# Indirect DMAs of GpSimd for the rows of the feed-forward layers, with an accumulating scatter for the last sum

## The chip, the cores and the metric

The kernel runs on one core of one Trainium2 chip. The metric is device time in microseconds (us). The core has five engines with queues of their own: TensorE (PE), VectorE (DVE), ScalarE (ACT), GpSimd (POOL) and SyncE (SP, which here only issues DMAs).

## What is computed

The input x has 4 sequences of 1024 tokens of 256 float32 values. The reference is a residual chain of four layers:

```python
x = x + attention(layernorm(x))       # 16 heads of 16, rope, degree-4 polynomial scores, causal
x = x + ffn(layernorm(x))             # first feed-forward layer
x = x + silu(fftconv(layernorm(x)))   # long convolution over the batch axis of this layout: 4 taps
x = x + ffn(layernorm(x))             # second feed-forward layer, the same weights
```

The feed-forward layer is a mixture of 16 experts of 176 hidden units, of which each token uses its 6 likeliest by a softmax gate, and a shared expert of 352 units; each expert is `(silu(x @ w1g) * (x @ w1u)) @ w2`. The kernel computes all experts for all tokens and multiplies the hidden units by the combine weight, zero for an expert that isn't chosen.

## The kernel before

`attention` computes the first layer and stores it into x1 in DRAM. Then all engines meet at a barrier, and `feed_forward` does the other three layers.

**Tiles.** A feed-forward tile is 4 blocks of 128 tokens, one block from each sequence, with 256 values each: 512 KB. There are 8 such tiles (NT) in each feed-forward layer, so 16 in all (TT). The rows of tile n come from x1 for n < 8, else from x3, the result of the first feed-forward layer and the convolution.

**Chunks.** The hidden units of all experts are cut into 25 chunks of 128 (FC), 22 of them routed (FM). For chunk c, PE computes gate and up (`gate_up`, L1237, 12 matmuls of 128x512 as three products of high and low parts), ACT applies SiLU (L965), DVE multiplies by up (L1134) and by the combine weights `cbs` (L1137; no such factor in the last 3 chunks, L1139), ACT and DVE split the product into a high part `ah` (L969) and a low part `al` (L1143), and PE adds the second layer (`down`, L1253) one chunk later.

**Work spread over the chunks.** Between the chunks of tile n stand the prologue of tile n+1 and the epilogue of tile n-1. Prologue: statistics of `xp` in chunks 9 and 10 (L1083), the reciprocal deviation on POOL (`rstd_of`, L897 and L899), normalising `xp` in chunk 11 (L1075), transposes in chunks 12 and 14 (L1263), the split of the transposed rows (L946, L1092), gate logits, softmax and the choice of experts in chunks 16 to 24. Epilogue: the transposed result is added to the residual rows `xe` in chunks 4 and 6 (L1150). In a tile of the first layer ("convolution tile") `xe` is then normalised, POOL does the convolution (`convolve`, L908 to L916), ACT its SiLU in chunk 14, and DVE the sum in chunk 16 (L1194). In the second layer ("plain tile") the sum of L1150 is the output.

**SP's queue.** All DMAs are issued by SP in one order. `weights_out(n)` stores the combine weights of tile n (L833) and loads them back, broadcast, for chunks 0 to 2; then `turn(n)` loads the residual rows `xe` of tile n-1, loads the rows `xp` of tile n+1, loads `cbs` for chunks 3 to 20 (each when chunk c-3 is multiplied), stores `xe`, and loads `cbs` for chunk 21. Before the first tile SP loads `xp`, the identity, the gate weights, the taps and then the feed-forward weights chunk by chunk (`stage`), which ACT and DVE split during tile 0.

PE, DVE, ACT and POOL run the tiles as two straight ones, a loop of three pairs, two straight ones, a loop of two pairs, and two straight ones.

Of the kernel before, what the change touches and what calls it, by code (L numbers as in the profile page):

```python
# [18 lines left out]
ALU = mybir.AluOpType  # L19
AX = mybir.AxisListType  # L20

P = 128
# [11 lines left out]
ONE = 1  # L34
# [670 lines left out]
def feed_forward(nc, x1, w1, w2, gate, taps_in, ident_in, weights_t, x3, out):  # L705
# [5 lines left out]
    with ctx:  # L711
# [3 lines left out]
        def sem(name):  # L715
# [8 lines left out]
                  for c in range(FM)]  # L724
# [29 lines left out]
        pad = sb("f_pad", [P, 1])  # L754
        zero = sb("f_zero", [P, 1])
# [12 lines left out]
                   conv_link csilu x3 xp xe store link""".split()  # L768
# [35 lines left out]
        def _(sp):  # L804
# [3 lines left out]
            def load(to, n, second, name):  # L808

                sp.dma_start(to[:], rows(x3, n - NT) if second else rows(x1, n)).then_inc(s[name], 16)  # L810

            sp.sem_inc(s["store"], ONE)
            load(xp, 0, False, "xp")
# [27 lines left out]
            for c in range(RING, FC):  # L841
                if c < FM:
                    spread(0, c)
                if c + 1 < FC:
                    stage(c + 1)
                if c == 4:
                    sp.wait_ge(s["tx"], KE)
                    load(xp, 1, False, "xp")
# [24 lines left out]
            with sp.Fori(1, NT - 1) as n:  # L873
                turn(n, False, False, x3, True)
            turn(NT - 1, True, False, x3, True)
            turn(NT, True, False, x3, True)
            with sp.Fori(NT + 1, TT - 1) as n:
                turn(n, True, True, out, True)
            turn(TT - 1, True, True, out, False)
            turn(TT, True, True, out, False)  # L880
            sp.wait_ge(s["store"], ONE + 16 * TT)

        @block.gpsimd
        def _(pool):
# [34 lines left out]

            rstd_of(0, "pst", "peps", "prs", 0)  # L920

            def tile(n, parity, epilogue, prologue):
# [483 lines left out]
```

## Time and profile before

| | us |
|---|---|
| median of 3 runs | 2603.06 (2592.45 to 2606.33) |
| the profiled execution, its own time | 2598.01 |
| its span | 2596.3 |
| attention, from the span's start | to about 786 |
| feed-forward, 16 tiles | from about 786 to 2596.3 |
| PE busy in the span | 2329.8 |

The span is the profiled part of the execution; 1.7 us lie around it. The mean TensorE clock granted was 0.937 of full speed over the span. SP shows no busy time, since issuing a DMA isn't counted as busy. PE, DVE, ACT and POOL are given as busy time; a matmul of 128x512 shows about 0.4 us though two follow each other every 0.23 us, since they overlap.

### The profile page before, as it was taken

What the parts mean: (1) busy time and instruction counts of PE and PEld (TensorE: products, weight loads), DVE (VectorE), ACT (ScalarE), POOL (GpSimd) and SP (SyncE); (2) the same over time, 40 slices, a digit from 0 to 9 for tenths busy, and PEclk for the clock granted to TensorE, in tenths of its full rate; (3) what the DMA queues carried; (4) which work ended last, traced back from release to release, by engine and by line L of the source; (5) the groups of instructions that cost most, each with busy time, mean ns of one, the idle gap of its engine ahead of it and who ended that gap; (6) DMA issues with size and microseconds to landing.
All of it is one profiled execution on the core that took longest, in us unless ns stands there. A gap on an engine that the chain in (4) does not pass through costs nothing.

```text
span 2596.3 us, 32427 instructions
## 1 busy us (share of the span) xinstructions
PE 2329.8 (90%) x11472; PEld 1711.7 (66%) x11472; DVE 1484.4 (57%) x2605; ACT 1019.5 (39%) x1550; POOL 463.5 (18%) x590
## 2 busy tenths in 40 slices
PE   4776976786686999999999999999999999999998
PEld 3333533442334777787778778787888887888887
DVE  3656765755675655656465565656545454454554
ACT  2555655554463533233333323333333332333332
POOL 1434433443360002202020120202000000000000
PEclk8788888887787999999999999999999999999999
DMA  3133123213304421222212212221222212212121
GB/s 103 20 65 57 37 54 57 58 17 57 81 7 127 141 82 46 83 74 63 67 57 74 64 64 74 67 67 51 82 74 62 73 54 77 72 61 74 61 66 57
DMA packets 114098, 170.57 MB, mean 66 GB/s; under 512 B 18320, under 2 KB 58896, under 8 KB 113808
## 3 DMA queue, kind: packets, MB, share of 16 engines
q1 hardware_dynamic: 113936, 168.44, 23.3%
q8 instruction: 98, 1.61, 0.2%
q14 instruction: 64, 0.52, 0.1%
HBM read 130.10 MB, written 13.11 MB: 55 GB/s over the span
## 4 chain that ended last, share of the span: by engine, by line
PE 65%; DVE 3%; issue 1%; DMA 1%; ACT 0%; POOL 0%; DVEq 0%; ACTq 0%; POOLq 0%; SPq 0%
PE ffn_psum L1237 42%; PE ffn_psum L1253 21%; DVE xp L1075 1%; PE ffn_psum L1263 1%; PE ffn_psum L1290 1%; DVE pr L1137 1%; DVE al L1143 0%; DVE pr L1134 0%; DMA cbs<-weights_t 0%; PE ffn_psum L1273 0%; PE ffn_psum L1279 0%; DVE w1l L1058 0%; DMA xp<-x 0%; DMA weights_t<-z 0%; DVE w2l L1060 0%
## 5 line engine op out<-in xcount | busy, mean ns | idle before, releaser
L1237 PE MATMUL ffn_psum<-f_xh,w1h 128*128 128x512 f32 x1600 | 513.1, 401 | 8.6 <-issue 8.6
L1134 DVE TENSOR_TENSOR pr<-pr,ffn_psum 128x512 f32<-128x512 f32 x352 | 242.4, 689 | 485.4 <-PE ffn_psum L1237 422.7
L969 ACT ACTIVATE ah<-pr 128x512 fp32r<-128x512 f32 x400 | 252.6, 632 | 657.2 <-DVE pr L1137 599.7
L1237 PE MATMUL ffn_psum<-f_xl,w1h 128*128 128x512 f32 x1600 | 504.5, 396 | 0.0
L1237 PE MATMUL ffn_psum<-f_xh,w1l 128*128 128x512 f32 x1600 | 504.1, 396 | 0.0
L426 DVE TENSOR_TENSOR a<-a 128x1024 f32<-128x1024 f32 (+2 forms) x304 | 323.5, 1087 | 241.9 <-ACT a L330 240.8
L965 ACT ACTIVATE pr<-ffn_psum 128x512 f32<-128x512 f32 x400 | 238.8, 597 | 449.8 <-DVE al L1143 279.4
L330 ACT ACTIVATE a<-attn_psum 128x1024 f32<-128x1024 f32 (+1 forms) x320 | 290.6, 942 | 285.9 <-PE attn_psum L639 285.3
L1143 DVE TENSOR_TENSOR al<-pr,ah 128x512 fp32r<-128x512 f32 x400 | 284.8, 712 | 181.6 <-ACT ah L969 159.4
L1237 PEld LDWEIGHTS ffn_psum<-f_xl,w1h 128*128 128x128 f32 x1600 | 302.6, 189 | 74.5 <-issue 2.9
L1237 PEld LDWEIGHTS ffn_psum<-f_xh,w1l 128*128 128x128 f32 x1600 | 302.1, 189 | 72.0
L1237 PEld LDWEIGHTS ffn_psum<-f_xh,w1h 128*128 128x128 f32 x1600 | 295.4, 190 | 70.9 <-issue 7.2
L1253 PE MATMUL ffn_psum<-ah,w2h 128*128 128x512 f32 x800 | 319.1, 399 | 22.6 <-DVE al L1143 22.6
L1253 PE MATMUL ffn_psum<-ah,w2l 128*128 128x512 f32 x800 | 316.3, 395 | 0.0
L1253 PE MATMUL ffn_psum<-al,w2h 128*128 128x512 f32 x800 | 316.1, 395 | 0.0
L639 PE MATMUL attn_psum<-qt,kt 48*128 48x512 f32 (+3 forms) x768 | 148.4, 441 | 174.8 <-DMA kt<-sq 160.8
L897 POOL TENSOR_TENSOR f_rstd<-f_mv,f_eps 128x4 f32<-128x4 f32 x24 | 13.0, 541 | 1474.9 <-DVE f_mv L1064 1474.9
L639 PEld LDWEIGHTS attn_psum<-qt,kt 48*128 48x128 f32 x768 | 70.5, 205 | 297.5 <-DMA kt<-sq 164.5
L1137 DVE TENSOR_TENSOR pr<-pr,cbs 128x512 f32<-128x512 f32 x352 | 251.8, 715 | 25.5 <-DMA cbs<-weights_t 5.5
L298 POOL TENSOR_SCALAR_AFFINE_SELECT a<-a 128x256 f32<-128x256 f32 x256 | 180.0, 719 | 144.3 <-DVE a L426 134.8
L1253 PEld LDWEIGHTS ffn_psum<-ah,w2h 128*128 128x128 f32 x800 | 150.5, 188 | 68.0 <-DVE al L1143 31.9
L660 PE MATMUL attn_psum<-a,v 128*32 128x512 f32 (+3 forms) x1536 | 175.0, 546 | 7.0 <-POOL a L298 4.4
(157 smaller groups left out, 2028.8 us busy)
## 6 DMA issues: line engine op xcount, KB each, us to landing
cbs<-weights_t SPq DMA_DIRECT2D x128, 256.0 KB, 3.2
cbs<-weights_t SPq DMA_DIRECT2D x64, 224.0 KB, 2.9
cbs<-weights_t SPq DMA_DIRECT2D x64, 192.0 KB, 2.9
cbs<-weights_t SPq DMA_DIRECT2D x64, 160.0 KB, 2.5
qt<-sq SPq DMA_DIRECT2D x128, 64.0 KB, 2.3
kt<-sq SPq DMA_DIRECT2D x128, 64.0 KB, 2.3
xp<-x SPq DMA_DIRECT2D x16, 512.0 KB, 5.3
cbs<-weights_t SPq DMA_DIRECT2D x64, 128.0 KB, 2.8
```

The costliest lines, as they stand in the source:

```text
L298: last = pool.affine_select(out=d[:, :, k], in_=d[:, :, k], compare_op=ALU.is_ge, fill=0.0, base=0, pattern=[[0, 2], [1, P]], channel_mult ...
L330: act.activation(a[:, n % RA, :, 0:width(u)], S(n)[:, :, 0:width(u)], ACT.Square).then_inc(s_q1, 1)
L426: dve.tensor_tensor(t, t, t, ALU.mult).then_inc(s_a, 1)
L639: last = pe.matmul(S(n)[:, half, col:col + w], kt[lo:lo + 3 * D, unit % 2, c, j * P:(j + 1) * P], qt[lo:lo + 3 * D, unit % 2, c, tiles[0] ...
L660: last = pe.matmul(OT(qc)[32 * h:32 * h + 32, at_:at_ + w], v[:, b % 2, lo:lo + 32], a[:, (n - 1 + h // 2) % RA, h % 2, col:col + w], star ...
L965: act.activation(pr[:], GB(q), ACT.Silu).then_inc(s["silu"], 1)
L969: act.activation(ah[:, q % 2], pr[:], ACT.Copy).then_inc(s["ah"], 1)
L1134: dve.tensor_tensor(t, t, UB(q), ALU.mult).then_inc(s["p1"], 1)
L1137: dve.tensor_tensor(t, t, cbs[:, c % RING], ALU.mult).then_inc(s["p"], 1)
L1143: dve.tensor_tensor(al[:, q % 2], pr[:], ah[:, q % 2].bitcast(F32), ALU.subtract).then_inc(s["al"], 1)
L1237: last = pe.matmul(out, lhs(a, k), rhs(b, k), start=n == 0, stop=n == 3 * KE - 1)
L1253: last = pe.matmul(OB(m), w[:, c, m * P:(m + 1) * P], t[:, q % 2], start=c == 0 and j == 0, stop=c == FC - 1 and j == 2)
```

## The change

- SP no longer loads `xp`. POOL keeps a column of row numbers per block (`load_at`, 128 x 4, uint32), adds 128 to all of them for each tile (`next_index`), and gathers the rows with four indirect DMAs of 128 rows of 1 KB.
- SP no longer stores `xe`. POOL stores it with four scattering indirect DMAs, with row numbers of its own (`store_at`). For the second layer these accumulate onto `out`.
- For that, SP copies the residual rows of the tile from x3 to `out` in DRAM where it loaded them into `xe`, and DVE copies the second layer's result from PSUM into `xe` instead of adding it.
- At the start of the feed-forward part SP issues a copy of the whole of x1 into x3, as the first entry of its queue. Only the first scatter waits for it.
- POOL's tiles are written out one by one, not looped. DVE waits for 64 per tile on the rows' semaphore (four DMAs of 16), SP for 64 per tile on the stores'.

```diff
-            sp.sem_inc(s["store"], ONE)
-            load(xp, 0, False, "xp")
+            sp.dma_start(x3, x1).then_inc(s["init"], 16)
             sp.dma_start(ident[:], ident_in).then_inc(s["const"], 16)
...
-            def turn(n, loads_second, residual_second, store_to, prologue):
-                sp.wait_ge(s["store"], ONE + 16 * (n - 1))
-                load(xe, n - 1, residual_second, "xe")
-                if prologue:
-                    sp.wait_ge(s["tx"], KE * (n + 1))
-                    load(xp, n + 1, loads_second, "xp")
+            def turn(n, residual_second, prologue):
+                if not (isinstance(n, int) and n == 1):
+                    sp.wait_ge(s["store"], 16 * B * (n - 1))
+                if residual_second:
+                    sp.dma_start(rows(out, n - 1 - NT), rows(x3, n - 1 - NT)).then_inc(s["xe"], 16)
+                else:
+                    sp.dma_start(xe[:], rows(x1, n - 1)).then_inc(s["xe"], 16)
...
-                if store_to is x3:
-                    sp.wait_ge(s["x3"], n)
-                    sp.dma_start(rows(x3, n - 1), xe[:]).then_inc(s["store"], 16)
-                else:
-                    sp.wait_ge(s["x2"], 2 * n)
-                    sp.dma_start(rows(out, n - 1 - NT), xe[:]).then_inc(s["store"], 16)
...
+            def next_index(to):
+                pool.tensor_tensor(to[:], to[:], step[:], ALU.add).then_inc(s["index"], 1)
+
+            def gather(dram, indexed):
+                pool.wait_ge(s["index"], indexed)
+                for b in range(B):
+                    pool.indirect_dma_start(xp[:, b], None, flat(dram), bass.IndirectOffsetOnAxis(load_at[:, b:b + 1], 0)
+                                            ).then_inc(s["xp"], 16)
+
+            def scatter(dram, indexed, **how):
+                pool.wait_ge(s["index"], indexed)
+                for b in range(B):
+                    pool.indirect_dma_start(flat(dram), bass.IndirectOffsetOnAxis(store_at[:, b:b + 1], 0), xe[:, b], None,
+                                            **how).then_inc(s["store"], 16)
...
+            for n in range(TT + 1):
+                if n < TT - 1:
+                    pool.wait_ge(s["tx"], KE * (n + 1))
+                    if n >= 2:
+                        pool.wait_ge(s["store"], 16 * B * (n - 1))
+                    if n + 1 == NT:
+                        first_index(load_at)
+                    else:
+                        next_index(load_at)
+                    gather(x1 if n + 1 < NT else x3, 2 * n + 2 + (n == 0))
+                if 1 <= n <= NT:
                     rstd_of(1, "cst", "ceps", "crs", n - 1)
-                if prologue:
+                if n < TT - 1:
                     rstd_of(0, "pst", "peps", "prs", n + 1)
-                if epilogue == "conv":
+                if 1 <= n <= NT:
                     convolve(n - 1)
+                    pool.wait_ge(s["x3"], n)
+                elif n:
+                    pool.wait_ge(s["x2"], 2 * n)
+                if n:
+                    if n in (1, NT + 1):
+                        first_index(store_at)
+                    else:
+                        next_index(store_at)
+                    to = 2 * n + 3 if n < TT - 1 else n + TT + 1
+                    if n == 1:
+                        pool.wait_ge(s["init"], 16)
+                    if n <= NT:
+                        scatter(x3, to)
+                    else:
+                        scatter(out, to, compute_op=ALU.add)
...
-                    dve.wait_ge(s["xp"], 16 * m + 16)
+                    dve.wait_ge(s["xp"], 16 * B * (m + 1))
...
-                dve.tensor_tensor(t, t, X.rearrange("p (b e) -> p b e", e=E), ALU.add).then_inc(s["x2"], 1)
+                y = X.rearrange("p (b e) -> p b e", e=E)
+                if plain:
+                    dve.tensor_copy(t, y).then_inc(s["x2"], 1)
+                else:
+                    dve.tensor_tensor(t, t, y, ALU.add).then_inc(s["x2"], 1)
```

## Rows read from the trace of the kernel before

**Rows 1.** The page, parts 1 and 4: busy time, and the chain's shares.
```profile
PE 2329.8 (90%) x11472; PEld 1711.7 (66%) x11472; DVE 1484.4 (57%) x2605; ACT 1019.5 (39%) x1550; POOL 463.5 (18%) x590
...
PE 65%; DVE 3%; issue 1%; DMA 1%; ACT 0%; POOL 0%; DVEq 0%; ACTq 0%; POOLq 0%; SPq 0%
```

**Rows 2.** Windows, convolution tile and plain tile: length, busy, clock, DMA share, GB/s.
```profile
1041.00:1152.00 111.00, 109.36 (x483) 87.98 (x482) 64.85 (x124) 37.50 (x62) 17.29 (x20) 1.00 0.22 68
...
1929.00:2038.00 109.00, 109.00 (x483) 88.23 (x482) 57.04 (x110) 36.76 (x62) 1.56 (x2) 1.00 0.22 68
```

**Rows 3.** Timeline at the feed-forward's start: start us, us, engine, what [idle before].
```profile
786.28 0.38 SPq L810 DMA_DIRECT2D xp<-x  x1
...
787.26 0.42 SPq L815 DMA_DIRECT2D pr<-gate  x1
...
790.78 1.41 DVE L1083 BATCH_NORM_STATS2 f_stats<-xp 128x6 f32<-128x256 f32 x4 [7.23 <-DMA xp<-x]
...
791.18 0.32 ACT L936 ACTIVATE gt_h<-pr 128x144 fp32r<-128x144 f32 x1 [12.32 <-DMA pr<-gate]
...
794.08 1.38 DVE L1075 TENSOR_SCALAR xp<-xp,f_mv,f_rstd 128x256 f32<-128x256 f32 x4 [1.28 <-POOL f_rstd L899]
...
794.59 0.26 ACT L983 ACTIVATE z<-z 128x64 f32<-128x64 f32 x1
...
796.73 0.60 ACT L946 ACTIVATE f_xh<-ffn_psum 128x512 fp32r<-128x512 f32 x1 [1.88 <-PE ffn_psum L1263]
```

**Rows 4.** Timeline of SP's queue: the combine weights' store, three tiles.
```profile
2147.21 0.31 SPq L833 DMA_DIRECT2D weights_t<-z  x1
...
2260.93 0.31 SPq L833 DMA_DIRECT2D weights_t<-z  x1
...
2369.72 0.31 SPq L833 DMA_DIRECT2D weights_t<-z  x1
```

**Rows 5.** Timeline where PE, DVE and ACT jump back in their loops.
```profile
1264.05 0.40 SPq L810 DMA_DIRECT2D xp<-x  x1
...
1270.12 0.69 DVE L1143 TENSOR_TENSOR al<-pr,ah 128x512 fp32r<-128x512 f32 x1 [5.02 <-issue]
```

**Rows 6.** Windows of two heavy loading stretches; last columns DMA share, GB/s.
```profile
4.00:8.00 4.00, 0.00 (x0) 0.00 (x0) 3.12 (x15) 0.00 (x0) 1.82 (x6) 1.00 1.09 410
...
788.00:790.00 2.00, 0.00 (x0) 0.00 (x0) 0.00 (x0) 0.00 (x0) 0.00 (x0) 0.50 0.94 308
```

**Rows 7.** The page, part 6: KB of one, median us from issue to landing.
```profile
xp<-x SPq DMA_DIRECT2D x16, 512.0 KB, 5.3
...
cbs<-weights_t SPq DMA_DIRECT2D x128, 256.0 KB, 3.2
...
affine<-ln_affine SPq DMA_DIRECT2D x8, 0.1 KB, 7.5
...
x<-xr SPq DMA_DIRECT2D x16, 256.0 KB, 2.3
```

**Rows 8.** Timeline of a plain tile: residual rows loaded, and first used.
```profile
1934.16 0.41 SPq L810 DMA_DIRECT2D xe<-x  x1
...
1952.84 0.68 DVE L1150 TENSOR_TENSOR xe<-xe,ffn_psum 128x512 f32<-128x512 f32 x1
```

**Rows 9.** Timeline of a convolution tile: Pool's first work, DVE's last sum.
```profile
1074.80 0.56 POOL L897 TENSOR_TENSOR f_rstd<-f_mv,f_eps 128x4 f32<-128x4 f32 x1 [81.47 <-DVE f_mv L1064]
...
1114.11 1.22 DVE L1194 TENSOR_TENSOR xe<-xe,z 128x1024 f32<-128x1024 f32 x1
```

**Rows 10.** Timeline: the four normalising instructions, convolution tile, then plain tile.
```profile
1090.82 3.19 DVE L1075 TENSOR_SCALAR xp<-xp,f_mv,f_rstd 128x256 f32<-128x256 f32 x4
...
2091.40 1.38 DVE L1075 TENSOR_SCALAR xp<-xp,f_mv,f_rstd 128x256 f32<-128x256 f32 x4
```

**Rows 11.** Timeline of the kernel's end.
```profile
2592.37 0.69 DVE L1150 TENSOR_TENSOR xe<-xe,ffn_psum 128x512 f32<-128x512 f32 x1 [1.20 <-PE ffn_psum L1290]
...
2593.09 0.39 SPq L867 DMA_DIRECT2D out<-xe  x1
```

More of the change, by code:

```diff
@@ L754, in feed_forward @@
         pad = sb("f_pad", [P, 1])
+        load_at = sb("load_at", [P, B], mybir.dt.uint32)
+        store_at = sb("store_at", [P, B], mybir.dt.uint32)
+        step = sb("step", [P, B], mybir.dt.uint32)
         zero = sb("f_zero", [P, 1])
@@ L767, in feed_forward @@
                    lgT lgS lgX sm ex comb cx cT cw g u silu p1 p ah al s2 oT back x2 cst ceps crs cy plink clink mx
-                   conv_link csilu x3 xp xe store link""".split()
+                   conv_link csilu x3 xp xe store link index init""".split()
         s = {n: sem("f_" + n) for n in names}
@@ L871, in turn @@
                     weights_out(n + 1)
[L873 to L876, printed above, removed]
+            turn(1, False, True)
+            with sp.Fori(2, NT + 1) as n:
+                turn(n, False, True)
             with sp.Fori(NT + 1, TT - 1) as n:
[L878 to L881, printed above, removed]
+                turn(n, True, True)
+            turn(TT - 1, True, False)
+            turn(TT, True, False)
+            sp.wait_ge(s["store"], 16 * B * TT)
         @block.gpsimd
@@ L918, in convolve, with first_index @@
                         links = links + 1
-            rstd_of(0, "pst", "peps", "prs", 0)
-            def tile(n, parity, epilogue, prologue):
-                if epilogue == "conv":
+            flat = lambda dram: dram.rearrange("b t p e -> (b t p) e")
+            def first_index(to):
+                pool.iota(to[:], [[N, B]], base=0, channel_multiplier=1).then_inc(s["index"], 1)
+            def next_index(to):
+                pool.tensor_tensor(to[:], to[:], step[:], ALU.add).then_inc(s["index"], 1)
@@ new lines, in _ @@
+            pool.iota(step[:], [[0, B]], base=P, channel_multiplier=0).then_inc(s["index"], 1)
+            first_index(load_at)
+            gather(x1, 2)
+            rstd_of(0, "pst", "peps", "prs", 0)
+            for n in range(TT + 1):
[4 more added lines that the diff above has]
+                    if n + 1 == NT:
+                        first_index(load_at)
+                    else:
+                        next_index(load_at)
+                    gather(x1 if n + 1 < NT else x3, 2 * n + 2 + (n == 0))
+                if 1 <= n <= NT:
@@ L924, in tile @@
                     rstd_of(1, "cst", "ceps", "crs", n - 1)
-                if prologue:
+                if n < TT - 1:
                     rstd_of(0, "pst", "peps", "prs", n + 1)
-                if epilogue == "conv":
+                if 1 <= n <= NT:
                     convolve(n - 1)
-            tiles(pool, tile)
+                    pool.wait_ge(s["x3"], n)
[13 more added lines that the diff above has]
+                        scatter(out, to, compute_op=ALU.add)
@@ L1143, in low_act, with residual @@
                 dve.tensor_tensor(al[:, q % 2], pr[:], ah[:, q % 2].bitcast(F32), ALU.subtract).then_inc(s["al"], 1)
-            def residual(e, half):
+            def residual(e, half, plain):
                 if half == 0:
@@ L1176, in tile @@
                     if epilogue and c in (4, 6):
-                        residual(n - 1, (c - 4) // 2)
+                        residual(n - 1, (c - 4) // 2, epilogue == "plain")
                     if epilogue == "conv":
@@ L1213, in _ @@
             for half in range(2):
-                residual(TT - 1, half)
+                residual(TT - 1, half, True)
         @block.tensor
```

5 lines of the change are left out of this document (removed).

## The prediction, on record before the changed kernel ran

> **What bounds the kernel now.** I read the page's busy shares and its chain first: PE is busy for 90% of the span and makes up 65% of the chain that ended last, and POOL has none of the chain [rows 1]. Then the windows of one tile of each kind: PE is busy for all 109 us of a plain tile, and for 109.36 of 111 us of a convolution tile, while the DMA engines are busy for 0.22 of it [rows 2]. So in the steady part only what makes PE wait counts, and moving rows on another queue changes nothing unless something arrives late. PE isn't the bound in three places: at the start of the feed-forward part [rows 3], where the loops jump back [rows 4, 5], and at the end [rows 11]. The change touches all three.
>
> **1. The copy of x1 into x3, first in SP's queue.** It is 4 x 8 x 128 x 256 float32 values, 4.19 MB, from DRAM to DRAM. Nobody waits for it until the first scatter, after chunk 16 of tile 1: that chunk is at 1114.1 us in tile 2 [rows 9], one tile of 110.8 us earlier in tile 1, so at 1003 us, 217 us after the start. By its own semaphore it is hidden. But behind it in the same queue stand the identity, the gate weights, the taps and the first chunks of w1 and w2, and the trace shows that a small transfer in this queue lands with the large ones ahead of it: the affine rows, 0.1 KB each, took 7.5 us at the median, where 256 KB took 3.2 us elsewhere [rows 7], and the gate weights were waited for until 791.18, 3.9 us after their issue, behind the 512 KB of `xp` [rows 3]. So I take it that the first weights arrive after the copy.
>
> How long is the copy? The highest rate shown is 410 GB/s, for loads from DRAM [rows 6]. The copy passes DRAM twice for each byte, so I halve it: 205 GB/s, 20.5 us. Nothing in the trace copies DRAM to DRAM, so the bounds are wide: at the full 410 GB/s 10.2 us, and at the slope between 256 KB in 3.2 us and 512 KB in 5.3 us (125 GB/s) [rows 7] 33.5 us. The latter two move pieces of 2 and 1 KB, the copy long runs, so I stay near the first.
>
> What is then late? The load of `xp` leaves this queue; at 308 GB/s [rows 6] it held it for 1.7 us. The weights move by 20.5 - 1.7 = 18.8 us. Behind them are two chains [rows 3]. Gate weights: ACT splits them at 791.18, DVE subtracts, and only then may it normalise; before, it sat idle for 1.28 us there, waiting for POOL, so 18.8 - 1.3 = 17.5 us remain. First w1 and w2: ACT splits them and the taps until 794.85, and starts on the transposed rows at 796.73, so there the slack is 1.9 us and 16.9 remain. The later one counts: **+17.5 us**, bounds +7.2 and +30.5 (10.2 and 33.5 less 3.0). Tile 0 can't win it back, since every stage of it follows these splits.
>
> The Trainium skill speaks on this. Its page "DMA: Bandwidth & Descriptors", section "Latency and other measured facts", gives copies between DRAM tensors 207 GB/s in each direction where the pitch isn't unlucky, and 103 to 164 where it is. By the first the copy would take 20.3 us and the sum stays; by the second 26 to 41 us, and the sum grows by 5 to 20 us. No row of this trace can decide between them.
>
> **2. The first gather.** POOL first writes three small constants and the row numbers, then issues four DMAs. The price of an indirect DMA on POOL is not in this trace. From below it is SP's issue of a plain one, 0.4 us [rows 3]; from above I put four times POOL's shortest step on two operands, 0.56 us [rows 9], so about 2 us, and rival D says what more would do. I take 1 us each. Then `xp` lands near 786.5 + 1 + 4 + 5 = 796.5 us, 6 us later than before. It lies under the 18.8 us of the gate weights, and costs nothing; without that cover it would be 4.5 us (6 less the 1.3 us).
>
> **3. Gathers and scatters in the steady part.** In a convolution tile x3's sum is ready at 1115.3 [rows 9]. POOL then adds to its row numbers, issues four scatters, waits for them to land, adds again and issues four gathers. What is queued behind these on POOL is the `rstd_of` of the convolution in the next tile, which DVE waits for: it comes at 1074.8 plus one tile of 110.8, so 1185.6 us. There are 70 us for eight DMAs and one landing of about 5.3 us: 13 us at 1 us each. In a plain tile the scatter follows chunk 10 and the gather chunk 14, and there are more than 80 us until the next chunk 10. `xp` is overwritten after its last transpose, as before, and the statistics need it in chunk 9 of the next tile. Cost 0, covered by PE's chunks; if the cover is gone, rival D.
>
> DVE and POOL do hinder each other: the four normalising instructions took 3.19 us beside POOL's convolution and 1.38 us in a plain tile, where POOL is idle [rows 10], and the convolution tile is the one in which PE idles 1.64 us [rows 2]. In plain tiles the scatter's four DMAs would now be issued just when chunk 11 normalises. If writing them hinders as the convolution does, it costs up to 1.64 us in each of 7 plain tiles, 11.5 us; if not, 0. POOL reads only 128 x 4 row numbers for it, so I go near the low end: **+2 us**.
>
> **4. SP's queue in the steady part.** In the first layer it loses the 512 KB of `xp`, at the place where the loops jump back. There DVE waited 5.02 us for its own instructions with this load just issued [rows 5], and the tile with the jump lasts 113.72 us where the next lasts 108.79 [rows 4]; 4.9 us more; there are three jumps. 512 KB are 1.7 us of the queue. If all of it delays the fetch, 3 x 1.7 = 5 us come back; if none, 0. I take **-1.5 us**. In the second layer the load of `xe` becomes a copy of the same size from x3 to out. It is issued at 1934.16 and first needed at 1952.84 [rows 8]: 18.7 us for a transfer that took 5.3 us as a load; twice that is still covered. DVE's copy out of PSUM replaces an addition with the same operand from PSUM: 0.
>
> **5. The end.** Before, the last addition ends at 2593.06, SP stores 512 KB, and the span ends at 2596.3, 3.2 us later [rows 11]. Now POOL waits for DVE, adds to its row numbers (0.56 us, the like at L897 [rows 9]), issues four DMAs at 1 us, and the last one has to land: 2.3 us as the 256 KB store [rows 7], more for reading first, say 3. Sum 7.6 instead of 3.2: **+4.5 us**. Bounds: +1 (0.4 us each, 2.3 to land: 4.4 less 3.2) and +10 (2 us each, 4.6 to land).
>
> **Sum.** 17.5 + 2 - 1.5 + 4.5 = +22.5 us on the profiled execution's 2598.0, so 2620.5. The median of the runs shown is 5.05 us above that execution, so the time is 2603.06 + 22.5 = **2625.6 us**, slower by 0.9%. All low ends together (7.2 + 0 - 5 + 1) give +3, all high ends (30.5 + 11.5 + 0 + 10) +52.
>
> **The rivals.**
> A. *The copy doesn't hold up the weights*, because it is fast or because the engines take from it only in between. This is the one on the other side: not slower. Then the first gather decides the start (+4.5, less up to 1.7 of queue time), and with the end the sum is 4.5 + 2 - 1.5 + 4.5 = +9.5, 2612.6 us, within 0.5%. It decides from where the delay is under 8 us, so the copy under 11 us or 380 GB/s. For it: 410 GB/s was seen. Against it: that was one pass through DRAM, and the order of landing in [rows 7].
> B. *The stall at the jumps goes away with `xp`'s load.* Three times 4.9, 14.8 us, in place of 1.5: +9.2, 2612.3 us, also within 0.5%. Against it: the five loads of `cbs` and the load of `xe` stay ahead of the fetch. Together with A it would be 2599 us, 0.1% faster, which no measurement tells.
> C. *The copy runs on few engines.* Its outermost dimension is 4, so if the transfer is cut along it, four engines of 16 carry it, at a quarter of the rate: 41 us at 410 GB/s to 82 us at 205. The delay is then 38 to 79 us and the time 2646 to 2687 us; middle 2666. Against it: both sides are one contiguous run, which may be cut in any way. The Trainium skill, page "DMA: Bandwidth & Descriptors", section "Rules for kernel authors", has this as a rule: an outermost dimension under 16 confines a DMA to that many engines. No DMA in this trace shows it.
> D. *POOL can't write its DMAs fast enough.* From 8.1 us for each ((70.3 - 5.3) / 8) the next `rstd_of` is late. At 10 us each it would be 15 us in each of 7 convolution tiles: +105, about 2730 us. For it: nothing but that the price is unknown.
> E. *Writing the DMAs hinders DVE's normalising* as the convolution does: 11.5 in place of 2, so 2635 us. The Trainium skill, page "SBUF — State Buffer", section "SBUF: two separate sides", says that one blocks the other, and that it is the DMA that waits behind DVE; by it the cost here is only a later scatter, and the sum would be 2 us less.
>
> **How the numbers follow.** Chances: forecast 0.60, A 0.13, B 0.05, A and B together 0.03, C 0.07, E 0.09, D 0.03. Change of 0.5% is 13 us, about what a measurement of this kernel tells from none. Slower by more: the forecast (all but 0.04 of it, for a copy near its lower bound), C, D and E, 0.75. Within it: A, B, both, and the 0.04, less 0.02, so 0.23. Faster by more: those 0.02, for both together with low ends elsewhere. Range: at the low end A and B reach to 2609; at the top the copy at its upper bound gives 2639, with E 2648, and C begins at 2646, so I go to 2655. Outside are D, most of C, and A and B together: under 2 in 10.
>
> **What would show it.** In the changed kernel's profile: a gap of about 30 us without PE from 783 us, ended by ACT waiting for the gate weights near 810 us (A: near 792, and DVE waiting for `xp`); SP's row of the copy with about 20 us to landing; tiles of 108.8 and 110.8 us as before; four normalising instructions in a plain tile of 1.4 us (E: 3.2); DVE's wait at the jump of 4 to 5 us (B: none); 7 to 8 us from the last copy of DVE to the end. The prediction is wrong above all if the weights are not held by the copy, or held much longer than 20 us.

## The result, and the profile after

The changed kernel takes 2614.03 us (median of 12 runs, 2605.38 to 2623.97), the kernel before 2602.94 (median of 12, 2592.45 to 2608.29): a ratio of 1.0047 with the interval [1.0027, 1.0066]. It is slower by 11 us (7 to 17). The forecast was 22.5 us slower; the time lies in the range, near its low end, and just inside "within 0.5%", a case that the forecast had given 0.23, against 0.75 for slower by more. It is also nearer to rival A's 2612.6 us than to the forecast's 2625.6, so the time alone can't say which of them is true; the profiles can.

Time was lost in two places, the start and the end, and little changed between them. To see that, the span is cut at events that both kernels have. The zero is the barrier between attention and feed-forward (POOL's first memset after it). Attention isn't touched by the change, yet its end lies between 779 and 792 us in the profiles of this study, so spans and single times carry up to 13 us that have nothing to do with an edit; stretches counted from the barrier don't.

| us | before | after | difference |
|---|---|---|---|
| barrier | 786.20 | 779.48 | -6.7 |
| barrier to DVE's statistics of `xp` | 4.58 | 16.70 | +12.1 |
| barrier to ACT's split of the gate weights | 4.98 | 17.09 | +12.1 |
| barrier to PE's first transpose | 9.41 | 21.50 | +12.1 |
| barrier to the first store of combine weights | 24.99 | 35.44 | +10.45 |
| tile 0, store to store | 115.61 | 115.32 | -0.3 |
| tiles 1 to 14 | 1551.76 | 1551.09 | -0.7 |
| the rest, to the end of DVE's last instruction | 114.50 | 114.35 | -0.15 |
| from there to the span's end | 3.24 | 10.72 | +7.5 |
| feed-forward, barrier to end | 1810.10 | 1826.92 | +16.8 |

By these profiles the feed-forward part is 16.8 us longer; the medians of whole runs say 11.1, with an interval that reaches 17. The profiles of the other runs weren't kept, so what lies between the two numbers isn't shown.

The page of the changed kernel, busy times (part 1), the queue of POOL's DMAs (part 3) and the chain's shares (part 4); [rows 1] are those of before:

```profile
PE 2315.5 (89%) x11472; PEld 1703.2 (65%) x11472; DVE 1485.1 (57%) x2605; ACT 1019.6 (39%) x1550; POOL 630.8 (24%) x751
...
q0 software_dynamic: 9216, 16.79, 2.8%
...
PE 64%; DVE 3%; issue 1%; DMA 1%; POOL 0%; ACT 0%; POOLq 0%; DVEq 0%; ACTq 0%
```

POOL does 167 us more work, and almost none of it is in the chain. The timeline of the changed kernel at the feed-forward's start, against [rows 3]:

```profile
779.49 0.59 SPq L811 DMA_DIRECT2D x<-x  x1
...
780.55 1.19 POOL L920 DMA_INDIRECT xp<-x,load_at  x1 [0.40 <-POOL load_at L912]
780.75 1.28 SPq L813 DMA_DIRECT2D pr<-gate  x1
782.04 0.96 POOL L920 DMA_INDIRECT xp<-x,load_at  x1 [0.30 <-issue]
...
784.56 0.95 POOL L920 DMA_INDIRECT xp<-x,load_at  x1 [0.30 <-issue]
796.18 1.41 DVE L1117 BATCH_NORM_STATS2 f_stats<-xp 128x6 f32<-128x256 f32 x4 [19.34 <-DMA xp<-x,load_at]
796.57 0.32 ACT L970 ACTIVATE gt_h<-pr 128x144 fp32r<-128x144 f32 x1 [25.93 <-DMA pr<-gate]
...
799.45 1.38 DVE L1109 TENSOR_SCALAR xp<-xp,f_mv,f_rstd 128x256 f32<-128x256 f32 x4 [1.25 <-POOL f_rstd L888]
...
800.98 1.08 PE L1301 MATMUL ffn_psum<-f_ident,xp 128*128 128x128 f32 x4 [24.93 <-DVE xp L1109]
```

Two things are late: ACT waits for the gate weights (the issue at 780.75), and DVE for the gathered `xp`, although the gathers stand in POOL's own queue and were issued by 785.5. The one that decides is `xp`. Before it normalises, DVE still waits 1.25 us for POOL's reciprocal deviation, as before (1.28 in [rows 3]), and that hangs on the statistics of `xp`; the gate weights have been used by then. The landings (the page's DMA issues: KB, median us) say the same, against [rows 7]:

```profile
out<-x SPq DMA_DIRECT2D x8, 512.0 KB, 4.6
...
xp<-x,load_at POOLq DMA_INDIRECT x64, 3.2
...
x<-xe,store_at POOLq DMA_INDIRECT x32, 2.5
out<-xe,store_at POOLq DMA_INDIRECT x32, 4.7
...
pr<-gate SPq DMA_DIRECT2D x1, 72.0 KB, 15.8
...
x<-x SPq DMA_DIRECT2D x1, 15.5
```

The copy landed 15.5 us after its issue: 4.19 MB / 15.5 us = 270 GB/s. The gate weights landed after it. Windows of the same stretch (us, PE, PEld, DVE, ACT, POOL, clock, DMA share, GB/s): the DMA share is 1 or more for 8 us, then the rate falls to 124 GB/s. A share of 1.40 can't be meant as it stands, so I take 507 GB/s as a matter of how a window counts long pieces, and only the whole landing as a rate.

```profile
779.50:783.50 4.00, 0.00 (x0) 0.00 (x0) 0.00 (x0) 0.00 (x0) 2.91 (x11) 0.50 0.74 264
783.50:787.50 4.00, 0.00 (x0) 0.00 (x0) 0.00 (x0) 0.00 (x0) 1.71 (x2) 0.50 1.40 507
787.50:791.50 4.00, 0.00 (x0) 0.00 (x0) 0.00 (x0) 0.00 (x0) 0.00 (x0) 0.50 1.01 314
791.50:795.50 4.00, 0.00 (x0) 0.00 (x0) 0.00 (x0) 0.00 (x0) 0.00 (x0) 0.50 0.41 124
```

Timeline of the end, against [rows 11]:

```profile
2594.99 0.69 DVE L1186 COPY xe<-ffn_psum 128x512 f32<-128x512 f32 x1 [1.06 <-PE ffn_psum L1328]
2595.77 0.19 POOL L915 TENSOR_TENSOR store_at<-store_at,step 128x4 uint32<-128x4 uint32 x1 [73.58 <-DVE xe L1186]
2596.24 1.55 POOL L926 DMA_INDIRECT out<-xe,store_at  x1 [0.28 <-POOL store_at L915]
...
2601.81 1.55 POOL L926 DMA_INDIRECT out<-xe,store_at  x1 [0.30 <-issue]
```

From DVE's last copy (2595.68) it takes 0.56 us to the first DMA, 7.12 us to issue four (4 x 1.55 + 3 x 0.30), and 3.04 us until the span ends.

The steady part: a plain tile at the place of the second row of [rows 10], then POOL's work after the sum that [rows 9] end with, in a convolution tile, and last DVE at a loop jump.

```profile
2092.71 1.69 POOL L926 DMA_INDIRECT out<-xe,store_at  x1 [0.29 <-POOL store_at L915]
...
2093.58 1.38 DVE L1109 TENSOR_SCALAR xp<-xp,f_mv,f_rstd 128x256 f32<-128x256 f32 x4
...
2094.70 2.30 POOL L926 DMA_INDIRECT out<-xe,store_at  x1 [0.30 <-issue]
...
1119.72 1.06 POOL L926 DMA_INDIRECT x<-xe,store_at  x1 [0.29 <-POOL store_at L915]
...
1126.98 0.56 POOL L915 TENSOR_TENSOR load_at<-load_at,step 128x4 uint32<-128x4 uint32 x1 [2.38 <-DMA x<-xe,store_at]
...
1131.62 1.30 POOL L920 DMA_INDIRECT xp<-x,load_at  x1 [0.30 <-issue]
...
1273.06 0.69 DVE L1177 TENSOR_TENSOR al<-pr,ah 128x512 fp32r<-128x512 f32 x1 [4.51 <-issue]
```

DVE normalises in 1.38 us, as before, while POOL writes DMAs. POOL's are the longer ones: the four of this tile take 1.69, 2.30, 1.98 and 1.54 us, where each of the last four of the kernel, with DVE idle, took 1.55. The first lies beside the normalising; the second shares only 0.26 us with it, and the rest with DVE's other work. The scatter, its landing and the gathers take 13.2 us, of 70 that are free. The last row is the wait at a loop jump, 4.51 us where [rows 5] have 5.02.

### The profile page after: what moved, and what is told of

Read it like the earlier page. It is cut to its first block, busy times and chain, and to the rows that moved or that the text cites. A ratio compares the mean times of both kernels' runs of the same rounds, so it can differ in the third digit from the quotient of the medians.

```text
span 2606.4 us, 32437 instructions
## 1 busy us (share of the span) xinstructions
PE 2315.5 (89%) x11472; PEld 1703.2 (65%) x11472; DVE 1485.1 (57%) x2605; ACT 1019.6 (39%) x1550; POOL 630.8 (24%) x751
## 3 DMA queue, kind: packets, MB, share of 16 engines
q0 software_dynamic: 9216, 16.79, 2.8%
HBM read 134.29 MB, written 21.50 MB: 60 GB/s over the span
## 4 chain that ended last, share of the span: by engine, by line
PE 64%; DVE 3%; issue 1%; DMA 1%; POOL 0%; ACT 0%; POOLq 0%; DVEq 0%; ACTq 0%
PE ffn_psum L1275 42%; PE ffn_psum L1291 21%; DVE xp L1109 1%; PE ffn_psum L1301 1%; PE ffn_psum L1328 1%; DVE pr L1171 1%; DVE al L1177 0%; DMA xp<-x,load_at 0%; DVE pr L1168 0%; DMA cbs<-weights_t 0%; PE ffn_psum L1317 0%; DVE w1l L1092 0%; PE ffn_psum L1311 0%; POOL out L926 0%; DVE w2l L1094 0%
## 5 line engine op out<-in xcount | busy, mean ns | idle before, releaser
L293 POOL TENSOR_TENSOR a<-a 128x256 f32<-128x256 f32 x128 | 119.3, 932 | 308.2 <-ACT a L330 308.1
```

Of the source, the lines that this page charges most:

```text
L293: pool.tensor_tensor(d, d, d, ALU.mult).then_inc(s_ad1, 1)
```

## The experiments

Each was profiled and, but for the last, timed against the kernel before. "FFN" is the stretch from the barrier to the end: 1810.10 before, 1826.92 after. The columns are stretches of the table above: three from the barrier, two between stores, and the end from DVE's last instruction.

| kernel | statistics | gate split | PE start | tile 0 | tiles 1 to 14 | end | FFN | ratio to before |
|---|---|---|---|---|---|---|---|---|
| before | 4.58 | 4.98 | 9.41 | 115.61 | 1551.76 | 3.24 | 1810.10 | |
| after | 16.70 | 17.09 | 21.50 | 115.32 | 1551.09 | 10.72 | 1826.92 | 1.0047 [1.0027, 1.0066] |
| e1 | 17.12 | 17.59 | 21.95 | 115.61 | 1554.05 | 3.18 | 1822.72 | 1.0034 [1.0015, 1.0052] |
| e2 | 8.33 | 2.99 | 13.13 | 119.06 | 1550.01 | 10.78 | 1822.15 | 1.0045 [1.0025, 1.0065] |
| e3 | 17.15 | 17.50 | 21.95 | 115.99 | 1550.64 | 3.23 | 1821.65 | 1.0037 [1.0018, 1.0055] |
| e4 | 8.19 | 3.12 | 12.98 | 117.11 | 1549.52 | 3.23 | 1812.18 | 1.0014 [0.9997, 1.0032] |
| e5 | 17.08 | 17.42 | 21.88 | 115.54 | 1551.28 | 7.72 | 1824.54 | 1.0026 [1.0006, 1.0045] |
| e6 | 16.92 | 16.53 | 21.72 | 115.46 | 1550.89 | 10.75 | 1826.79 | 1.0046 [1.0025, 1.0066] |
| e7 | 4.48 | 4.89 | 9.30 | 115.80 | 1539.13 | 3.20 | 1797.27 | 0.9930 [0.9907, 0.9953] |
| e8 | 13.63 | 6.50 | 18.42 | 115.40 | 1550.37 | 10.80 | 1822.95 | 1.0047 [1.0026, 1.0067] |
| e9 | 13.13 | 18.58 | 20.69 | 115.44 | 1551.48 | 10.85 | 1827.12 | 1.0078 [1.0048, 1.0108] |
| e10 | 4.47 | 4.86 | 9.30 | 115.73 | 1538.90 | 2.52 | 1796.27 | 0.9952 [0.9934, 0.9970] |
| e11 | 8.23 | 2.92 | 13.03 | 115.81 | 1538.08 | 3.22 | 1800.25 | 0.9942 [0.9921, 0.9962] |
| e12 | 14.12 | 14.52 | 18.95 | 115.59 | 1553.84 | 3.20 | 1819.52 | one run |

The ratios lie up to 0.3% from what FFN says, and their intervals are some 0.2% (5 us) to each side: they tell none of e1, e2, e3, e5, e6 and e8 from the changed kernel, and for e5 what FFN says (+14.4 us, 0.55%) lies outside the interval. So the steps are read from the stretches, each of one profile. In every kernel but e9, PE starts 4.8 us after the statistics of `xp`: the column "statistics" decides the start, and the gate weights only in e9.

### The copy alone, in the kernel before (e1)

```diff
+            sp.dma_start(x3, x1).then_inc(s["init"], 16)
             sp.sem_inc(s["store"], ONE)
...
+            sp.wait_ge(s["init"], 16)
             with sp.Fori(1, NT - 1) as n:
```

> The kernel before, with only the copy of x1 into x3 added as the first entry of SP's queue (SP waits for it before tile 1). Theory (the copy is passed through by everything behind it in SP's queue; it took 15.5 us to land in the changed kernel): xp, gate weights and first weights all come about 15.5 us later, PE's first transposes 15 us later, less up to 1.6 us that PE won back at a higher granted clock: slower by 13 to 15 us. Rival (the copy only shares the engines, the change's loss is elsewhere): under 4 us.

PE starts 12.5 us later than before and the end is as before. That is less than the 15 expected: `xp` is used 1.3 us after the copy has landed (15.8), where before it took 4.5 from its issue, so part of its way passes beside the copy. The copy by itself gives a start as late as the changed kernel's. Tiles 1 to 14 are 2.3 us longer; 2.0 of that lie in the three tiles with a jump (345.12 us together, 343.16 before), as again in e12 (345.19). No run tells why.

### Only a quarter of the copy, late (e2)

The scatters overwrite tiles 0 to 5 of x3 before anything gathers from it, so only tiles 6 and 7 are copied, and that is issued in tile 0. By the kernel's code even these copied rows are never read, since a tile of x3 is gathered six tiles after its own scatter; no run leaves the copy out of the changed kernel altogether.

```diff
-            sp.dma_start(x3, x1).then_inc(s["init"], 16)
...
+                if c == 4:
+                    sp.dma_start(x3[:, NT - 2:], x1[:, NT - 2:]).then_inc(s["init"], 16)
```

> The changed kernel with the copy cut to the quarter of x1 that the later tiles haven't yet stored (4 pieces of 256 KB, tiles 6 and 7) and moved behind chunk 4's weights of tile 0. Theory: the start is then decided by the four gathers, whose last lands about 8.3 us after the barrier against 4.5 us for xp before; so 7 to 9 us faster than the changed kernel, about 2606 us, 3 to 4 us slower than the kernel before plus what the end costs (7.5). Rival (the gathers are what is late at the start): no faster than the changed kernel by more than 2 us.

The gate weights are split at 2.99 us, and now the gathered `xp` is last: 8.33 us where SP's load of before took 4.58. That is the price of the gathers without the copy, +3.7 us at PE's start. But 7 to 9 us less than the changed kernel were expected, and the ratio shows no gain: in FFN 7.2 us are won until the first store and 3.7 lost again in tile 0, which is 3.5 us longer than before. The section on e12 takes this up.

### The last tile stored by SP (e3), and both (e4)

```diff
-                if residual_second:
+                if isinstance(n, int) and n == TT:
+                    sp.dma_start(xe[:], rows(x3, n - 1 - NT)).then_inc(s["xe"], 16)
+                elif residual_second:
...
-            sp.wait_ge(s["store"], 16 * B * TT)
+            sp.wait_ge(s["x2"], 2 * TT)
+            sp.dma_start(rows(out, NT - 1), xe[:]).then_inc(s["last"], 16)
+            sp.wait_ge(s["store"], 16 * B * (TT - 1))
+            sp.wait_ge(s["last"], 16)
...
-            for n in range(TT + 1):
+            for n in range(TT):
...
-                residual(TT - 1, half, True)
+                residual(TT - 1, half, False)
```

The last two hunks are POOL without its last scatter, and DVE adding the last tile's residual rows again. e4 is this edit and that of e2.

> The changed kernel with the last tile's sum and store done as before: SP loads its residual rows, DVE adds, SP stores. Theory: the end goes from 10.7 us after DVE's last instruction back to 3.2 us, so 7.5 us faster than the changed kernel. Rival (end is covered or a matter of the profile): 0 to 2 us.

> Both edits. Theory: the two costs add, so what is left against the kernel before is the gathers' 3 to 4 us at the start less about 1 us in the tiles: ratio 1.000 to 1.002. Rival (a third cost in the steady part, hidden so far): above 1.003.

With SP's store the end is 3.23 us: the scatter had cost all of the 7.5. FFN of e3 is only 5.3 us under the changed kernel's, since from PE's start to the first store it took 15.8 us, as before, and not 13.9; the granted clock rose later (below). With both edits FFN is 1812.18, 2.1 us over before: +3.2 until the first store, tile 0 +1.5, the rest -2.6. No third cost shows.

### A plain scatter in the second layer (e5)

```diff
-                    sp.dma_start(rows(out, n - 1 - NT), rows(x3, n - 1 - NT)).then_inc(s["xe"], 16)
+                    sp.dma_start(xe[:], rows(x3, n - 1 - NT)).then_inc(s["xe"], 16)
...
-                        scatter(out, to, compute_op=ALU.add)
+                        scatter(out, to)
...
-                        residual(n - 1, (c - 4) // 2, epilogue == "plain")
+                        residual(n - 1, (c - 4) // 2, False)
...
-                residual(TT - 1, half, True)
+                residual(TT - 1, half, False)
```

> The changed kernel, but in the second layer too SP loads the residual rows into xe, DVE adds them, and the four scatters store without accumulating. The copy stays. Theory: an accumulating scatter costs POOL 1.55 us each against 0.96 us and lands later (3.4 to 5 us against 2.5), and only the last tile's four lie on the path: the end after DVE shrinks from 10.7 to about 7.5 us, the rest is as in the changed kernel, 3 us faster than it. Rival (accumulating costs in the steady part too, by traffic or by hindering DVE): plain tiles shorter than 108.7 us, 5 us or more in all.

The end is 7.72 us, so accumulating is 3.0 of the 7.5 and going by POOL at all is 4.5. The plain tiles last 108.8 us as in the changed kernel, so accumulating costs nothing there. The groups of the scatter's line (ns, min/median/max) in the changed kernel, both forms, and in this one:

```profile
L926 POOL DMA_INDIRECT x<-xe,store_at x32: 956/970/1063, 1009.1 to 1795.2; - x32
L926 POOL DMA_INDIRECT out<-xe,store_at x32: 1541/1690/2327, 1875.2 to 2601.8; - x32
```

```profile
L926 POOL DMA_INDIRECT out<-xe,store_at x32: 959/976/1181, 1884.1 to 2609.3; - x32
```

POOL's queue here has 6144 packets, against 9216 in the changed kernel for the same bytes: 48 for a plain DMA of 128 rows (6144 / 128), and 144 for an accumulating one ((9216 - 96 x 48) / 32).

### The copy on ACT's queue (e6), in short pieces (e8), short pieces on SP's (e9)

If the weights wait because they stand behind the copy in SP's queue, another queue frees them.

```diff
-            sp.dma_start(x3, x1).then_inc(s["init"], 16)
...
+            act.dma_start(x3, x1).then_inc(s["init"], 16)
             act.wait_ge(s["const"], 32)
```

> The changed kernel with the same whole copy issued by ACT, in a queue of its own, at the same moment. Theory (order in SP's queue is what holds the weights): the two queues share the engines, so gate weights land some 3 us after the barrier plus at most as much again, and the gathers at 8.3 us or a little later decide: PE starts 13 to 16 us after the barrier instead of 21.5, total 5 to 8 us less. Rival (bandwidth is what holds them, or long pieces are not interrupted): PE starts at 20 us or later, no gain.

That theory fell: the gate weights are split 16.53 us after the barrier, 0.6 us earlier than in the changed kernel, and the statistics come 0.2 us later. (The identity, issued at the same moment as the copy, landed in 1.8 us; the gate weights, 0.4 us behind it, did not.) The copy's queue and landings in e6:

```profile
q10 hardware_dynamic: 80, 4.19, 0.5%
...
pr<-gate SPq DMA_DIRECT2D x1, 72.0 KB, 16.1
...
x<-x ACTq DMA_DIRECT2D x1, 15.8
```

80 packets for 4.19 MB: pieces of about 64 KB. So what if a piece, once begun, holds its engine, whatever the queue? e8 is e6 with `max_dma_last_dim=2048` on the copy (pieces of 2 KB), e9 the changed kernel with it.

> The changed kernel with the copy issued by ACT in a queue of its own, as in the run before, but cut into pieces of 2 KB in place of 64 KB (2048 in place of 64 pieces). The run with long pieces on ACT's queue held the weights as much as on SP's, so order in SP's queue was not what held them. Theory now (an engine works a long piece off before it takes a piece of another queue): with short pieces the queues take turns, the gate weights and xp land within 10 us of the barrier, PE starts at 13 to 16 us instead of 21.5, the store of the first combine weights at 28 to 31 us instead of 35.4. Rival (the 4.2 MB hold the memory or the engines whatever their pieces): PE starts at 20 us or later.

> The changed kernel with the copy first in SP's queue, as it was, in pieces of 2 KB. Theory (both hold: inside one queue the order counts, between queues the length of pieces): the weights still come after the copy, gate weights 16 us or more after the barrier, but the gathers, on POOL's queue, land at about 9 us. Rival (only the length counts): gate weights within 10 us too, PE starts at 13 to 16 us.

e8, the same rows, and its timeline:

```profile
q10 hardware_dynamic: 2064, 4.19, 0.5%
...
x<-x ACTq DMA_DIRECT2D x1, 4096.0 KB, 19.4
...
pr<-gate SPq DMA_DIRECT2D x1, 72.0 KB, 6.1
```

```profile
793.85 0.32 ACT L970 ACTIVATE gt_h<-pr 128x144 fp32r<-128x144 f32 x1 [15.35 <-DMA pr<-gate]
800.48 0.63 ACT L975 ACTIVATE w1h<-xe 128x512 fp32r<-128x512 f32 x1 [6.31 <-DMA back<-w]
800.98 1.41 DVE L1117 BATCH_NORM_STATS2 f_stats<-xp 128x6 f32<-128x256 f32 x4 [16.26 <-DMA xp<-x,load_at]
```

With 2064 packets in place of 80 the gate weights are split at 6.50 us (16.53 in e6): the length of the pieces had held them, not the order of the queue. But the larger transfers are still late beside the copy: w1 comes 13.1 us after the barrier, the gathers 13.6, and PE starts at 18.42, 3.1 us earlier than in the changed kernel, where 13 to 16 were expected. In e9, short pieces ahead in SP's own queue, the gate weights wait until 18.58, and the gathers, on POOL's queue, come at 13.13, not at the 9 expected. There the gate weights decide: DVE waits for them, and PE starts 2.1 us after their split. From its timeline:

```profile
792.03 4.52 SPq L812 DMA_DIRECT2D f_ident<-ident  x1
...
809.96 0.32 ACT L970 ACTIVATE gt_h<-pr 128x144 fp32r<-128x144 f32 x1 [27.39 <-DMA pr<-gate]
810.32 0.31 DVE L1193 TENSOR_TENSOR gt_l<-pr,gt_h 128x144 fp32r<-128x144 f32 x1 [3.98 <-ACT gt_h L970]
```

So both are true: behind the copy in the same queue one waits for all of it (it landed 18.1 us after its issue in e9); in another queue one waits for long pieces, and with short ones small transfers come early and larger ones late. That the latter share the rate with the copy is my reading; no run varies it.

### Where a quarter copy runs (e12)

```diff
+            sp.dma_start(x3[:, NT - 2:], x1[:, NT - 2:]).then_inc(s["init"], 16)
             sp.sem_inc(s["store"], ONE)
...
+            sp.wait_ge(s["init"], 16)
             with sp.Fori(1, NT - 1) as n:
```

> The kernel before, with a copy of only the last quarter of x1 into x3 (tiles 6 and 7: 4 runs of 256 KB, 1.05 MB, the outermost dimension 4) as the first entry of SP's queue; nothing else is changed, and nothing needs the copy. Disputed: whether a copy whose outermost dimension is 4 and whose sides are not one contiguous run is carried by few engines (rival C), which e2_late_quarter hinted at with a tile 0 that was 3.5 us longer. If all 16 engines carry it at the 270 GB/s of the whole copy, it lands about 4 to 6 us after its issue and the gate weights are split about 7 to 8.5 us after the barrier (4.98 before, 17.6 with the whole copy alone). If 4 engines carry it at a quarter of that rate, it lands after about 16 us, DMA share stays near 0.3 to 0.5 at some 130 GB/s of reading and writing, and the gate weights are late by as much as with the whole copy if they stand behind it on those engines, so about 17 us; with four engines at a higher rate each, something between, 9 to 13 us.

A copy of a quarter of the bytes delays PE's start by 9.5 us, where the whole one in the same place (e1) delays it by 12.5. The gate weights are split at 14.52 us: far from the 7 to 8.5 of 16 engines at the full rate, between the two expectations for four. The packets of SP's queue, of the kernel before, of e1 and of e12:

```profile
q1 hardware_dynamic: 113936, 168.44, 23.3%
```

```profile
q1 hardware_dynamic: 114016, 172.64, 24.1%
```

```profile
q1 hardware_dynamic: 113956, 169.49, 23.4%
```

80 packets more for the whole copy, 20 for the quarter. If a piece is 64 KB, these are 64 and 16 pieces and 16 and 4 packets more, one for each engine that takes part: 16 and 4 engines, 4 pieces each. That is my reading of the counts; what supports it is the time, which falls by a quarter when the bytes fall to a quarter. Windows of e12:

```profile
782.50:784.50 2.00, 0.00 (x0) 0.00 (x0) 0.00 (x0) 0.00 (x0) 0.35 (x6) 0.50 0.33 102
784.50:788.50 4.00, 0.00 (x0) 0.00 (x0) 0.00 (x0) 0.00 (x0) 0.00 (x0) 0.50 0.76 255
788.50:792.50 4.00, 0.00 (x0) 0.00 (x0) 0.00 (x0) 0.00 (x0) 0.00 (x0) 0.50 0.49 171
792.50:796.50 4.00, 0.00 (x0) 0.00 (x0) 0.00 (x0) 0.00 (x0) 0.00 (x0) 0.50 0.39 114
```

From 788.5 on, half and more of the engines' time is free, and `xp` and the gate weights still don't land until 796.6. The same 20 packets (97060, against 97040 in e6's queue of SP) were issued in tile 0 of e2 at 819.05, and a later w1 and w2 were waited for:

```profile
835.16 0.63 ACT L976 ACTIVATE w1h<-xe 128x512 fp32r<-128x512 f32 x1 [1.86 <-DMA back<-w]
```

e4 has the same copy in the same place and the same wait (1.38 us), but its tile 0 is only 1.5 us longer than before, not 3.5. The windows tell the two apart: after the wait the granted clock of e2 is 0.91 and 0.67 of full speed in 836 to 840 and 840 to 844, so it was at 1.2 GHz for some 3.4 us, which costs 1.7; in e4 it stays at 2.4 GHz. So the copy costs tile 0 some 1.5 us, and the fall of the clock behind the idle PE came on top in one of two profiles.

### The loops unrolled (e7), and versions that beat both kernels (e10, e11)

The changed kernel writes out only POOL's tiles. e7 is the kernel before with all of PE's, DVE's, ACT's and POOL's written out; e10 adds the last store in two halves; e11 is the changed kernel with these tiles written out, the last tile stored by SP, and the copies of tiles 6 and 7 one at a time in tile 0, as rows of 1 KB with 128 of them outermost.

```diff
-            tile(0, 0, None, True)
...
+            for n in range(TT):
+                tile(n, n % 2, None if n == 0 else "conv" if n <= NT else "plain", n < TT - 1)
```

Only in e11:

```diff
+                if c in (4, 12):
+                    t = NT - 2 if c == 4 else NT - 1
+                    sp.dma_start(rows(x3, t), rows(x1, t)).then_inc(s["init"], 16)
```

> The kernel before with the 16 tiles of PE, DVE, ACT and POOL written out one by one instead of looped (the change did this for POOL alone). Theory: only the three jumps back cost, 3.6, 4.1 and 4.9 us in the trace of before; without them 12 us faster, 0.995. Rival (longer code is fetched late everywhere): no gain or slower.

> The kernel before with all 16 tiles of PE, DVE, ACT and POOL written out (as in the run that gave 0.993), and the last store cut in two, the first half sent when DVE has added it. Theory: the jumps' 12.6 us as there, and the end after DVE 2.3 to 2.8 us in place of 3.2: ratio 0.993 to 0.995, at or a little under the unrolled one. Rival (the second store waits for the first, or the gain of the unrolled one was partly luck): 0.996 or more.

> The changed kernel without its three costs: the copy cut to the rows of tiles 6 and 7 in pieces of 1 KB over all engines and sent after the weights of chunks 4 and 12; the last tile's sum and store as before; the tiles of PE, DVE and ACT written out. Gathers and the other scatters stay on POOL. Theory (moving the rows costs nothing in the tiles and 3 to 4 us at the start): 3 us slower than the kernel before unrolled, ratio 0.994 to 0.996. Rival (a hidden cost of the gathers and scatters in the tiles): tiles longer than 108.8 and 110.8 us.

e7 gains 12.8 us in FFN (ratio 0.9930): tiles 1 to 14 lose 12.6, the three jumps. e10 is at 1796.27 the shortest FFN; its split store takes 0.7 us off the end. e11 is 3.0 us behind e7: PE starts 3.7 later (the gathers), and its tiles 1 to 14 are 1.1 shorter. The two copies of one tile each cost tile 0 nothing (115.81), where the single one cost e2 3.5 and e4 1.5. By their ratios, whose intervals overlap, e7, e10 and e11 can't be told apart.

## Why the prediction was half right

**Step 1, the copy.** The place was right, the size and the path were wrong. In size the step that failed is halving the loading rate: the copy ran at 270 GB/s, not 205, and landed after 15.5 us, not 20.5. The Trainium skill's 207 GB/s for copies between DRAM tensors with a row pitch of 512 KB ("DMA: Bandwidth & Descriptors", section "Latency and other measured facts") is below what this contiguous copy measured, which decides. With 15.5 the step's own working gives 15.5 - 1.7 - 1.3 = 12.5 where PE's start measured 12.1, and that this fits is luck. By the working the gate weights come 13.8 us late and DVE's idle time before normalising takes up 1.3 of it. They came 12.1 us late, and that idle time is still there (1.25 us), since it hangs on the statistics of `xp`. What PE waited for was the gathered `xp`, 12.1 us late too. The gate weights weren't last: with the 2.1 us from their split to PE's start that e9 shows, they alone would have let PE start at 19.2 us (an estimate) and not at 21.5, so their slack before was 2.3 us, not 1.3.

The reason given was incomplete too: I had only the order of SP's queue, but e6 shows that the copy's long pieces hold the weights from another queue just as well. And "tile 0 can't win it back" was wrong by 1.6 us: from PE's start to the first store it is 15.58 us before and 13.94 after. The granted clock was at 2.4 GHz sooner after PE began: windows give 0.71 for 806 to 812 before, where PE had started at 795.61, and 0.87 for 808 to 812 after, start 800.98; a mix of 0.5 and 1.0 puts the rise at 809.5 and 809.0, so 13.9 and 8.1 us behind the start. It doesn't follow from the late start: e3 starts PE as late (21.95), its clock rises 14.4 us behind that (0.83 for 824 to 828), and nothing is won back (15.80). No run tells why.

**Step 2, the first gather.** The term was put at 0 beside the copy, and this is the step that had the path wrong: the gathers were to land 10 us after the start, under the cover of the weights, but landed at 16.7 and were the last thing that PE's start waited for. The copy's long pieces held them, though they stand in POOL's queue; one took up to 13.9 us to land, where 3.2 is the median. By the estimate above this made PE start 2.3 us later than the weights alone. Without the copy their price was put at 4.5 us and measured 3.6 to 3.7 (e2, e4, e11). That it is near comes of two errors that cancel in part: they landed at 8.3 us, not 10, and the 1.3 us that were taken off (6 less 1.3 would be 4.7) lie behind the statistics and absorb nothing.

**Step 3, the steady part.** The DMAs are 0.96 us each and 0.30 us between (1 us assumed), scatter to last gather 13.2 us (13). The +2 beside normalising was nothing: DVE 1.38 us as before. By the Trainium skill's page "SBUF — State Buffer", section "SBUF: two separate sides", it is the DMA that waits behind DVE. The trace agrees in that DVE isn't slower and POOL's instructions are, up to 2.30 us for 1.55; but the longest lies mostly beside other work of DVE, and the one beside the normalising took 1.69. Rivals D and E are out. Together tiles 0 to 15 gained 1.1 us.

**Step 4, the jumps.** Forecast -1.5. The two profiles give -0.2: the three jump tiles last 342.92 us together, 343.16 before. All profiles together leave it open. The three kernels with `xp` on SP's queue have 343.16, 345.12 and 345.19 (before, e1, e12); the eight looped ones with the gathers on POOL have 341.2 to 343.1, 342.3 in the mean, and DVE's waits at the jumps are 4.51, 4.42 and 4.23 us in the changed kernel against 5.02, 5.57 and 4.94. So some 2 us may have come back, and since POOL's tiles are written out in the same kernels, no run tells whether by `xp`'s load or by that. B is out: most of the stall stays. It goes away when all engines' tiles are written out, with `xp`'s load where it was (e7). The copy from x3 to `out` lands in 4.6 us and is hidden.

**Step 5, the end.** Forecast +4.5, measured +7.5. The mis-sized term is "four DMAs at 1 us": an accumulating one takes POOL 1.55 and 0.30 us, so 7.1 in place of 4; the landing was 3.0 as assumed. e3 gives it all back, e5 gives back 3.0.

**The sum.** By the profiles +10.45 - 1.1 + 7.5 = +16.8 against +22.5: the start is 7.05 less than forecast, the steady part 1.6 less (-1.1 for 2 - 1.5), the end 3.0 more. The end's error hides part of the start's, so the total is nearer than the start alone; that is luck. The medians' 11.1 is half of the forecast; attention's length, which varies by up to 13 us, may stand between it and 16.8, and the interval [1.0027, 1.0066] holds both.

**Rivals A and C.** A asked for a copy under 11 us, or for engines that take from it only in between; e8 comes nearest to the second and still starts PE 9 us late. C is false for the whole copy, contiguous on both sides (270 GB/s, full DMA share), but e12 and the packet counts support it for the quarter. By the Trainium skill's rule on an outermost dimension under 16 ("DMA: Bandwidth & Descriptors", section "Rules for kernel authors") both would run on 4 engines; e12 agrees, if the packets are read rightly, and the whole copy doesn't. Where the quarter copy ended in time isn't seen, as nobody waited for it.

## What to carry to other kernels

Where PE is busy all the time, moving rows to another queue gains nothing; look only at the places where the kernel is bound by something else, and put no transfer that nobody needs yet ahead of, or beside, the first loads there: a long copy delayed them from both queues that were tried. Store the last tile by the shortest way, whatever serves the others. When two transfers are late together, look which wait ends last: the forecast priced the weights, and the gathers decided. And a loop whose jumps cost 4 us each is worth writing out before anything finer is tried: here it gave 12.8 us of the feed-forward part, where the whole change moved it by 16.8.

## What the runs showed of the hardware

- A contiguous DRAM to DRAM copy of 4.19 MB ran at 270 GB/s in 80 packets, and transfers of other queues waited for it: a 72 KB load issued 0.4 us behind it landed after 16.1 us (e6), gathers after up to 13.9, and only a load issued at the same moment came in 1.8 us. Cut into 2064 packets it took 19.4 us and let the 72 KB load through in 6.1 (e8).
- A quarter of it (e12), in four runs of 256 KB, delayed the loads behind it by 9.5 us, three quarters as much as the whole: 20 packets.
- Behind the copy of short pieces, SP's next issue took 4.52 us (e9); behind the long ones 0.57.
- An indirect DMA of 128 rows of 1 KB takes POOL 0.96 us and 0.30 until the next; accumulating, 1.55 and three times the packets (144 for 48), and 4.7 us to land where a plain one took 2.5.
